# A per-sample 64x64 product with residual add: a laid-out x and result, whole-bank moves, held-back loads and block-diagonal products

## The chip, the cores and the metric

The kernel runs on one core of one Trainium2 chip. The metric is the device time of one execution in microseconds (us). Lower is better.

## What is computed

```python
def _L0_cond_ref(x, conditions, weights):
    w = weights[conditions]
    return jnp.einsum('bct,bcd->bdt', x, w)
x = x + _L0_cond_ref(x, itok_B_1_198, L0_cond_weights)
```

x is 64 x 64 x 512 float32 (samples B, channels C, times T: 8.39 MB), the table of weights is 200 x 64 x 64 float32, and itok_B_1_198 holds one table index per sample. Each sample's 64x512 matrix is multiplied by the transpose of its own 64x64 weight matrix and added to itself. Both kernels fold the addition into the product by adding the identity to each gathered weight matrix. So 8.39 MB of x and 1.05 MB of weights are read, and 8.39 MB are written.

## The kernel before

**Tiling.** Two samples make a pair (PAIR = 2): the first sits on partitions 0 to 63, the second on 64 to 127, by channel. There are 32 pairs. Four pairs make a turn, so there are TURNS = 8 turns. Half a turn (two pairs, 512 KB) is a round; there are 16 rounds, and each has one load and one store. All of x fits in `x_sb` and all of the result in `y_sb`, so no load waits for a buffer.

**Weights.** The sample indices are loaded as one row by a DMA that the ScalarE queue issues (L91). VectorE (DVE) spreads them over partitions with four 32x32 transposes (L133) and computes a table row for each partition (L137). GpSimd (POOL) issues one indirect DMA (L103), the gather, which brings 8 KB to each of 128 partitions into `gathered`. DVE adds the identity on the diagonals (L143) and transposes 32x32 blocks into `w_all` (L146). In L146 it reads `gathered` with a step of 64 elements. The semaphore `w_ready` then lets TensorE (PE) start.

**Turns.** For each pair PE makes two matmul calls (L119), one per half h of the partitions, each with 64 rows by 64 columns of the array: half h of `x_sb` times half h of `w_all`. Sample h of a pair goes to the product tile h, and g, the pair's parity, chooses the half of the product's partitions. So four calls of the two pairs g = 0, 1 use four different quarters of the array. A float32 call is two MATMUL instructions in the trace. There are two sets of product tiles (SETS = 2), each of two tiles of two banks. PE waits for the moves of the turn two before.

**Moves.** ScalarE (ACT, L95) copies product tile 0 to `y_sb` partitions 0 to 63, DVE (L152) copies tile 1 to partitions 64 to 127. Each does it in two instructions per turn, one for each half g of the product's partitions, so an instruction moves 64 partitions x 1024 elements.

**Order of the transfers.** SyncE (SP) issues all 16 loads first with no wait (L80), then for each turn waits for the moves of both engines (L83, L84) and issues two stores (L85). All loads and stores are on this one queue in this order. x and the result stand in DRAM sample by sample, so that a transfer of one partition's part of one pair is a run of 2 KB. The last wait is for all stores.

Of the kernel before, what the change touches and what calls it, by code (L numbers as in the profile page):

```python
# [3 lines left out]


def conditioned_residual_kernel(nc: bass.Bass, x: bass.AP, conditions: bass.AP, weights: bass.AP, out: bass.AP):
# [8 lines left out]
    fp32 = mybir.dt.float32  # L15
# [3 lines left out]
    B, C, T = x.shape  # L19
    S, _, D = weights.shape  # L20
    PAIR = 2
    P = PAIR * C
    PAIRS = B // PAIR
    Q = 32
    K = C // Q
    ROUNDS = PAIRS // 2
    TURNS = ROUNDS // 2
    SETS = 2

    x_rows = x.rearrange("(n two) c t -> (two c) n t", two=PAIR)  # L30
    out_rows = out.rearrange("(n two) c t -> (two c) n t", two=PAIR)
    condition_row = conditions.rearrange("b one -> one b")
    table = weights.rearrange("s (k c) d -> (s k) (c d)", k=K)

    ctx = ExitStack()
    with ctx:  # L36
# [13 lines left out]
        gathered = sbuf("gathered", [P, Q * D], fp32)  # L50
        w_all = sbuf("w_all", [P, D, PAIRS], fp32)

# [3 lines left out]
        x_loaded = [semaphore(f"x_loaded{m}") for m in range(ROUNDS)]  # L56
# [4 lines left out]
        rows_known = semaphore("rows_known")  # L61
        w_gathered = semaphore("w_gathered")
        identity_added = semaphore("identity_added")
        w_ready = semaphore("w_ready")
        multiplied = semaphore("multiplied")
# [8 lines left out]
        def slots_of(turn, g):  # L74
            return slice(4 * turn + g, 4 * turn + 4, 2)
# [12 lines left out]
        @block.scalar  # L88
        def _(act):
            act.wait_ge(condition_cleared, 1)  # L90
            act.dma_start(condition[0:1, :], condition_row).then_inc(condition_loaded, 16)  # L91
# [14 lines left out]

        @block.tensor
        def _(pe):
            pe.wait_ge(w_ready, 1)
            for turn in range(TURNS):  # L110
                if turn >= SETS:
                    pe.wait_ge(moved_by_act, 2 * (turn - SETS + 1))
                    pe.wait_ge(moved_by_dve, 2 * (turn - SETS + 1))
                for j in range(2):
                    pe.wait_ge(x_loaded[2 * turn + j], 16)
                    for g in range(2):
                        for h in range(PAIR):
                            n = 4 * turn + 2 * j + g
# [52 lines left out]
```

## Time and profile before

| | us |
|---|---|
| median of 3 runs | 51.25 |
| lowest, highest | 50.74, 51.54 |
| the profiled execution, its own time | 50.88 |
| its span, first to last instruction | 49.1 |
| busy DVE / ACT / PE / POOL in it | 24.8 / 17.4 / 17.5 / 1.6 |
| bytes moved by DMA | 17.84 MB |

The profile is of one execution. Its span begins at the first instruction and ends at the last; 1.8 us of the execution's own time lie outside the span. Busy times count computing instructions only. L12 is line 12 of the kernel. PEld is the loading of weights into TensorE. The DMA share is the mean busy share of the core's 16 DMA engines; packets of one engine can overlap, so it may be a little over 1.

### The profile page before, as it was taken

To read this page: it belongs to the slowest core of one execution; us is meant where nothing else is said; L and a number is where in the kernel's file an instruction comes from. 1 tells how busy PE (TensorE), PEld (TensorE's weight loads), DVE (VectorE), ACT (ScalarE), POOL (GpSimd) and SP (SyncE) were. 2 spreads that over 40 slices of the span, in tenths; PEclk is the share of its full clock that TensorE was granted. 3 is DMA by queue.
4 is the path that set the end of the run, shared out by engine and by line. 5 is a ranking of instruction groups with operands and counts; after the bars stand their busy time and mean duration, and the time that the engine had idled before them with its cause. 6 is when DMAs were issued, how large, how long until landed. Compare 5 with 4: busy or idle time off the path is not lost.

```text
span 49.1 us, 383 instructions
## 1 busy us (share of the span) xinstructions
PE 17.5 (36%) x128; PEld 7.0 (14%) x128; DVE 24.8 (50%) x28; ACT 17.4 (35%) x17; POOL 1.6 (3%) x9
## 2 busy tenths in 40 slices
PE   0000000000000069997495959696969300000000
PEld 0000000000000023240333334343424000000000
DVE  1043000000089930059999999999999997000000
ACT  0720000000000000059977878796969690000000
POOL 4003500000000000000000000000000000000000
PEclk9999999999999999999999999999999999555555
DMA  0399999999999999999999999999999999999950
GB/s 0 68 382 406 350 361 334 417 409 429 386 397 401 386 389 384 389 386 391 382 389 392 411 404 402 414 407 404 407 411 406 404 404 406 404 406 412 402 199 13
DMA packets 8851, 17.84 MB, mean 364 GB/s; under 512 B 530, under 2 KB 530, under 8 KB 8722
## 3 DMA queue, kind: packets, MB, share of 16 engines
q1 hardware_dynamic: 8704, 16.78, 90.7%
q0 software_dynamic: 144, 1.05, 5.1%
q8 instruction: 1, 0.02, 0.1%
q10 hardware_dynamic: 2, 0.00, 0.0%
HBM read 9.44 MB, written 8.39 MB: 363 GB/s over the span
## 4 chain that ended last, share of the span: by engine, by line
DVE 45%; DMA 19%; issue 8%; PE 8%; DVEq 3%; POOL 1%; POOLq 1%
DVE y_sb L152 37%; DMA gathered<-weights,table_row 19%; PE product L119 8%; DVE w_all L146 7%; DVEq L36 3%; POOL piece L101 1%; DVE gathered L143 1%; POOLq L36 0%; POOLq L161 0%
## 5 line engine op out<-in xcount | busy, mean ns | idle before, releaser
L119 PE MATMUL product<-x_sb,w_all 64*64 64x512 f32 x128 | 17.5, 669 | 21.0 <-DVE w_all L146 17.6
L95 ACT COPY y_sb<-product 64x1024 f32<-64x1024 f32 x16 | 16.1, 1007 | 21.7 <-PE product L119 21.5
L152 DVE COPY y_sb<-product 64x1024 f32<-64x1024 f32 x16 | 19.6, 1223 | 4.3 <-PE product L119 3.8
L119 PEld LDWEIGHTS product<-x_sb,w_all 64*64 64x64 f32 x128 | 7.0, 204 | 30.7 <-DVE w_all L146 17.6
L143 DVE TENSOR_TENSOR gathered<-gathered,piece 128x64 f32<-128x64 f32 x1 | 0.3, 268 | 9.4 <-DMA gathered<-weights,table_row 9.4
L146 DVE STREAM_TRANSPOSE w_all<-gathered 128x2048 f32<-128x2048 f32 x1 | 3.6, 3621 | 0.0
L95 ACT ACT_TABLE_LOAD x1 | 1.3, 1283 | 1.5 <-DVE condition L126 1.5
L133 DVE STREAM_TRANSPOSE condition_of<-condition 32x32 int32<-32x32 int32 x4 | 0.8, 202 | 1.8 <-DMA condition<-conditions 1.7
L103 POOL DMA_INDIRECT gathered<-weights,table_row x1 | 1.1, 1068 | 3.2 <-DVE table_row L137 3.2
L126 DVE MEMSET condition<- 32x64 int32 x1 | 0.1, 112 | 0.8 <-PEq L161 0.8
L101 POOL MEMSET piece<- 32x1 f32 x4 | 0.4, 91 | 0.5 <-POOLq L161 0.3
L128 DVE MEMSET piece<- 32x1 f32 x4 | 0.2, 59 | 0.2
L137 DVE TENSOR_SCALAR table_row<-condition_of,piece 128x1 int32<-128x1 int32 x1 | 0.2, 214 | 0.1
L161 POOL MEMSET const-uint8-127<- 128x1 uint8 x1 | 0.1, 128 | 0.0
L161 POOL MEMSET const-bfloat16-1.0<- 128x1 bf16 x1 | 0.1, 123 | 0.0
L161 POOL MEMSET const-float32-1.0<- 128x1 f32 x1 | 0.1, 114 | 0.0
L161 POOL MEMSET const-float32-0.0<- 128x1 f32 x1 | 0.1, 103 | 0.2 <-issue 0.2
## 6 DMA issues: line engine op xcount, KB each, us to landing
x_sb<-x SPq DMA_DIRECT2D x16, 512.0 KB, 11.2
out<-y_sb SPq DMA_DIRECT2D x16, 512.0 KB, 5.8
condition<-conditions ACTq DMA_DIRECT2D x1, 0.2 KB
gathered<-weights,table_row POOLq DMA_INDIRECT x1, 9.1
```

The source lines that it names most:

```text
L36: with ctx:
L95: nc.scalar.copy(y_sb[halves(0), slots_of(turn, g), :], product[turn % SETS][0][halves(g), :, :]).then_inc(moved_by_act, 1)
L101: nc.gpsimd.memset(piece[q * Q:(q + 1) * Q, 0:1], float(1 - q % K)).then_inc(pieces_set, 1)
L103: nc.gpsimd.indirect_dma_start(gathered[:, :], None, table, bass.IndirectOffsetOnAxis(ap=table_row[:, 0:1], axis=0),).then_inc(w_gathered, 16)
L119: product_of = nc.tensor.matmul(product[turn % SETS][h][halves(g), j, :], w_all[halves(h), :, n], x_sb[halves(h), n, :], start=True, stop= ...
L128: nc.vector.memset(piece[q * Q:(q + 1) * Q, 1:2], float(q % K)).then_inc(pieces_set, 1)
L133: nc.vector.transpose(condition_of[q * Q:(q + 1) * Q, :], condition[:, q // K:B:PAIR]).then_inc(condition_turned, 1)
L137: nc.vector.tensor_scalar(table_row[:, :], condition_of[:, 0:1], float(K), piece[:, 1:2], ALU.mult, ALU.add).then_inc(rows_known, 1)
L143: nc.vector.tensor_tensor(diagonal, diagonal, piece[:, :].unsqueeze(1).to_broadcast([P, Q, K]), ALU.add).then_inc(identity_added, 1)
L146: nc.vector.transpose(w_all[:, :, :], gathered[:, :].rearrange("p (c d) -> p d c", d=D)).then_inc(w_ready, 1)
L152: nc.vector.tensor_copy(y_sb[halves(1), slots_of(turn, g), :], product[turn % SETS][1][halves(g), :, :]).then_inc(moved_by_dve, 1)
L161: nc = bacc.Bacc("TRN2", target_bir_lowering=False, num_devices=1)
```

## The change

The arrays are now laid out by the caller. x comes as [128 partitions, 32 pairs, 512], so that the four pairs of a turn are one run of 8 KB in each partition's row of 64 KB, and the result leaves in the same form. The table's rows are stored with d outside and c inside, so that the block transpose into `w_all` reads `gathered` in its own order. In the device kernel:

- **Transfers.** One load and one store per turn (1 MB each), 8 and 8 instead of 16 and 16. SP issues two loads, then waits for `gather_started`, which POOL's issue of the gather sets, and then issues the other six.
- **Moves.** One instruction per engine and turn: ACT moves product tile 0 and DVE product tile 1, each 128 partitions x 1024 elements.
- **Products.** Turns 0 to 3 (TILED = 4) as before, two calls of 64x64 for each pair. Turns 4 to 7 take one call for each pair, with a 128x128 weight matrix `w_diag` that holds the two samples' matrices as diagonal blocks. Its two other blocks are set to zero early, one by POOL (L113) and one by DVE (L150). ACT fills the diagonal blocks for turn t + 4 with two copies (L101) ahead of its move of turn t.
- **Waits.** PE waits for x once per turn, and in turns 4 to 7 also for `w_zeroed` and `w_placed`.

The diff, cut to its core:

```diff
-            for m in range(ROUNDS):
-                sp.dma_start(x_sb[:, 2 * m:2 * m + 2, :], x_rows[:, 2 * m:2 * m + 2, :]).then_inc(x_loaded[m], 16)
-            for m in range(ROUNDS):
-                if m % 2 == 0:
-                    sp.wait_ge(moved_by_act, m + 2)
-                    sp.wait_ge(moved_by_dve, m + 2)
-                sp.dma_start(out_rows[:, 2 * m:2 * m + 2, :], y_sb[:, 2 * m:2 * m + 2, :]).then_inc(stored, 16)
-            sp.wait_ge(stored, 16 * ROUNDS)
+            for turn in range(TURNS):
+                if turn == EARLY:
+                    sp.wait_ge(gather_started, 1)
+                sp.dma_start(x_sb[:, pairs_of(turn), :], x[:, pairs_of(turn), :]).then_inc(x_loaded[turn], 16)
+            for turn in range(TURNS):
+                sp.wait_ge(moved_by_act, turn + 1)
+                sp.wait_ge(moved_by_dve, turn + 1)
+                sp.dma_start(out[:, pairs_of(turn), :], y_sb[:, pairs_of(turn), :]).then_inc(stored, 16)
+            sp.wait_ge(stored, 16 * TURNS)
...
             for turn in range(TURNS):
+                if turn < TILED:
+                    later = slice(4 * turn, 4 * turn + 4)
+                    act.wait_ge(w_ready, 1)
+                    for h in range(PAIR):
+                        nc.scalar.copy(w_diag[halves(h), later, h * D:(h + 1) * D],
+                                       w_all[halves(h), :, pairs_of(TILED + turn)].rearrange("p d n -> p n d")
+                                       ).then_inc(w_placed, 1)
                 act.wait_ge(multiplied, turn + 1)
-                for g in range(2):
-                    nc.scalar.copy(y_sb[halves(0), slots_of(turn, g), :], product[turn % SETS][0][halves(g), :, :]
-                                   ).then_inc(moved_by_act, 1)
+                nc.scalar.copy(y_sb[:, 4 * turn:4 * turn + 2, :], product[turn % SETS][0][:, :, :]
+                               ).then_inc(moved_by_act, 1)
...
+            pool.wait_ge(pieces_set, 2 * (P // Q))
+            nc.gpsimd.memset(w_diag[halves(1), :, 0:D], 0.0).then_inc(w_zeroed, 1)
             pool.wait_ge(rows_known, 1)
             nc.gpsimd.indirect_dma_start(gathered[:, :], None, table,
                                          bass.IndirectOffsetOnAxis(ap=table_row[:, 0:1], axis=0),
-                                         ).then_inc(w_gathered, 16)
+                                         engine_sem=gather_started).then_inc(w_gathered, 16)
...
             for turn in range(TURNS):
+                pe.wait_ge(x_loaded[turn], 16)
                 if turn >= SETS:
-                    pe.wait_ge(moved_by_act, 2 * (turn - SETS + 1))
-                    pe.wait_ge(moved_by_dve, 2 * (turn - SETS + 1))
+                    pe.wait_ge(moved_by_act, turn - SETS + 1)
+                    pe.wait_ge(moved_by_dve, turn - SETS + 1)
+                if turn == TILED:
+                    pe.wait_ge(w_zeroed, 2)
+                if turn >= TILED:
+                    pe.wait_ge(w_placed, PAIR * (turn - TILED + 1))
                 for j in range(2):
-                    pe.wait_ge(x_loaded[2 * turn + j], 16)
                     for g in range(2):
+                        n = 4 * turn + 2 * j + g
+                        if turn >= TILED:
+                            product_of = nc.tensor.matmul(product[turn % SETS][j][:, g, :], w_diag[:, n - 4 * TILED, :],
+                                                          x_sb[:, n, :], start=True, stop=True)
+                            continue
                         for h in range(PAIR):
...
+            nc.vector.memset(w_diag[halves(0), :, D:PAIR * D], 0.0).then_inc(w_zeroed, 1)
...
-            diagonal = bass.AP(gathered, 0, [[Q * D, P], [D + 1, Q], [Q, K]])
+            diagonal = bass.AP(gathered, 0, [[D * Q, P], [Q + 1, Q], [Q * Q, K]])
...
-            nc.vector.transpose(w_all[:, :, :], gathered[:, :].rearrange("p (c d) -> p d c", d=D)
+            nc.vector.transpose(w_all[:, :, :], gathered[:, :].rearrange("p (d c) -> p d c", d=D)
...
-                for g in range(2):
-                    nc.vector.tensor_copy(y_sb[halves(1), slots_of(turn, g), :], product[turn % SETS][1][halves(g), :, :]
-                                          ).then_inc(moved_by_dve, 1)
+                nc.vector.tensor_copy(y_sb[:, 4 * turn + 2:4 * turn + 4, :], product[turn % SETS][1][:, :, :]
+                                      ).then_inc(moved_by_dve, 1)
```

On SP, the transfers stood before in this order (`x_sb<-x` is a load of one round, `out<-y_sb` a store; the first rows of the queue, up to the third turn's stores):

```order
L80 DMA x_sb<-x 128x2x512 x16
L85 DMA out<-y_sb 128x2x512 [waits moved_by_dve,moved_by_act]
L85 DMA out<-y_sb 128x2x512
L85 DMA out<-y_sb 128x2x512 [waits moved_by_dve,moved_by_act]
L85 DMA out<-y_sb 128x2x512
```

and now all of them are these:

```order
L85 DMA x_sb<-x 128x2048 x2
L85 DMA x_sb<-x 128x2048 [waits gather_started]
L85 DMA x_sb<-x 128x2048 x5
L89 DMA out<-y_sb 128x2048 [waits moved_by_dve,moved_by_act] x8
```

Six of the eight loads moved behind the gather's issue; nothing else is on SP's queue between them.

On ACT, the queue between its table load and the turn-1 move was before (`product_0` is product tile 0 of either set):

```order
L95 ACT_TABLE_LOAD
L95 COPY y_sb<-product_0 64x2x512 [waits multiplied]
L95 COPY y_sb<-product_0 64x2x512
L95 COPY y_sb<-product_0 64x2x512 [waits multiplied]
L95 COPY y_sb<-product_0 64x2x512
```

and now it is, with the placing of weights ahead of each of the first four moves:

```order
L101 ACT_TABLE_LOAD
L101 COPY w_diag<-w_all 64x4x64 [waits w_ready]
L101 COPY w_diag<-w_all 64x4x64
L105 COPY y_sb<-product_0 128x1024 [waits multiplied]
L101 COPY w_diag<-w_all 64x4x64 [waits w_ready]
L101 COPY w_diag<-w_all 64x4x64
L105 COPY y_sb<-product_0 128x1024 [waits multiplied]
```

On PE, the last two turns are now (`x2` is two calls in a row on the same tile):

```order
L135 MATMUL product_0<-x_sb,w_diag 128x512 [waits moved_by_dve,w_placed,moved_by_act,x_loaded6]
L135 MATMUL product_0<-x_sb,w_diag 128x512
L135 MATMUL product_1<-x_sb,w_diag 128x512 x2
L135 MATMUL product_0<-x_sb,w_diag 128x512 [waits moved_by_dve,w_placed,moved_by_act,x_loaded7]
L135 MATMUL product_0<-x_sb,w_diag 128x512
L135 MATMUL product_1<-x_sb,w_diag 128x512 x2
```

Four calls of 128 partitions stand in each where eight calls of 64 partitions stood.

## Rows read from the trace of the kernel before

**Rows 1.** The page's second part: busy tenths in 40 slices.
```profile
DVE  1043000000089930059999999999999997000000
...
DMA  0399999999999999999999999999999999999950
GB/s 0 68 382 406 350 361 334 417 409 429 386 397 401 386 389 384 389 386 391 382 389 392 411 404 402 414 407 404 407 411 406 404 404 406 404 406 412 402 199 13
```
**Rows 2.** Busy time by stretch; the last three columns are granted clock, DMA share, GB/s.
```profile
2.00:5.00 3.00, 0.00 (x0) 0.00 (x0) 1.02 (x5) 0.78 (x1) 0.50 (x1) 1.00 0.96 352
5.00:9.00 4.00, 0.00 (x0) 0.00 (x0) 0.00 (x0) 0.00 (x0) 0.57 (x1) 1.00 1.00 352
9.00:13.00 4.00, 0.00 (x0) 0.00 (x0) 0.00 (x0) 0.00 (x0) 0.00 (x0) 1.00 1.02 414
14.00:24.00 10.00, 5.42 (x36) 1.80 (x36) 6.15 (x4) 2.58 (x3) 0.00 (x0) 1.00 1.05 390
28.00:38.00 10.00, 8.04 (x71) 3.58 (x64) 9.75 (x9) 8.02 (x9) 0.00 (x0) 1.00 1.05 407
...
47.00:48.00 1.00, 0.00 (x0) 0.00 (x0) 0.00 (x0) 0.00 (x0) 0.00 (x0) 0.50 0.30 115
```
**Rows 3.** The page's third part: DMA queues (q1 is SP's, q0 the gather's).
```profile
q1 hardware_dynamic: 8704, 16.78, 90.7%
q0 software_dynamic: 144, 1.05, 5.1%
```
**Rows 4.** The page's sixth part: issues, KB each, us to landing.
```profile
x_sb<-x SPq DMA_DIRECT2D x16, 512.0 KB, 11.2
out<-y_sb SPq DMA_DIRECT2D x16, 512.0 KB, 5.8
gathered<-weights,table_row POOLq DMA_INDIRECT x1, 9.1
```
**Rows 5.** Groups of instructions: count, busy us, mean ns, idle before and its releaser.
```profile
L152 DVE COPY y_sb<-product 64x1024 f32<-64x1024 f32 x16 | 19.6, 1223 | 4.3 <-PE product L119 3.8
L119 PE MATMUL product<-x_sb,w_all 64*64 64x512 f32 x128 | 17.5, 669 | 21.0 <-DVE w_all L146 17.6 <-issue 2.5 <-ACT y_sb L95 0.9
L95 ACT COPY y_sb<-product 64x1024 f32<-64x1024 f32 x16 | 16.1, 1007 | 21.7 <-PE product L119 21.5
...
L146 DVE STREAM_TRANSPOSE w_all<-gathered 128x2048 f32<-128x2048 f32 x1 | 3.6, 3621 | 0.0
...
L128 DVE MEMSET piece<- 32x1 f32 x4 | 0.2, 59 | 0.2
...
L126 DVE MEMSET condition<- 32x64 int32 x1 | 0.1, 112 | 0.8 <-PEq L161 0.8
```
**Rows 6.** The timeline: start us, duration us, engine, line, what.
```profile
0.75 0.53 POOL L101 MEMSET piece<- 32x1 f32 x4 [0.29 <-POOLq L161]
0.76 16.83 SPq L80 DMA_DIRECT2D x_sb<-x  x16
...
2.99 0.90 DVE L133 STREAM_TRANSPOSE condition_of<-condition 32x32 int32<-32x32 int32 x4 [1.69 <-DMA condition<-conditions]
...
4.50 1.07 POOL L103 DMA_INDIRECT gathered<-weights,table_row  x1 [3.22 <-DVE table_row L137]
13.66 0.27 DVE L143 TENSOR_TENSOR gathered<-gathered,piece 128x64 f32<-128x64 f32 x1 [9.44 <-DMA gathered<-weights,table_row]
```
**Rows 7.** The timeline of TensorE's first two turns.
```profile
17.64 5.37 PE L119 MATMUL product<-x_sb,w_all 64*64 64x512 f32 x32 [17.64 <-DVE w_all L146]
18.57 0.25 PEld L119 LDWEIGHTS product<-x_sb,w_all 64*64 64x64 f32 x4 [0.59 <-issue]
...
20.28 0.25 PEld L119 LDWEIGHTS product<-x_sb,w_all 64*64 64x64 f32 x4 [0.60 <-issue]
...
21.56 0.21 PEld L119 LDWEIGHTS product<-x_sb,w_all 64*64 64x64 f32 x4 [0.22 <-issue]
21.99 0.21 PEld L119 LDWEIGHTS product<-x_sb,w_all 64*64 64x64 f32 x4 [0.22 <-issue]
...
23.95 2.01 PE L119 MATMUL product<-x_sb,w_all 64*64 64x512 f32 x16 [0.94 <-ACT y_sb L95]
```
**Rows 8.** The chain that ended last: its share by line, and its last piece.
```profile
by line: DVE y_sb L152 37.4%; DMA gathered<-weights,table_row 18.6%; issue 7.9%; PE product L119 7.6%; DVE w_all L146 7.4%; DVEq L36 2.5%; POOL piece L101 0.7%; DVE gathered L143 0.6%; POOLq L36 0.5%; POOLq L161 0.0%
...
40.18 1.23 DVE y_sb L152
```

More of the change, by code:

```diff
@@ L3, with conditioned_residual_kernel @@
 from contextlib import ExitStack
-def conditioned_residual_kernel(nc: bass.Bass, x: bass.AP, conditions: bass.AP, weights: bass.AP, out: bass.AP):
+PAIR = 2
+def conditioned_residual_kernel(nc: bass.Bass, x: bass.AP, conditions: bass.AP, table: bass.AP, out: bass.AP):
     fp32 = mybir.dt.float32
@@ L17, in conditioned_residual_kernel @@
     ALU = mybir.AluOpType
[L19 to L23, printed above, removed]
+    P, PAIRS, T = x.shape
+    B = conditions.shape[1]
+    C = D = P // PAIR
     Q = 32
     K = C // Q
-    ROUNDS = PAIRS // 2
-    TURNS = ROUNDS // 2
+    TURNS = PAIRS // 4
     SETS = 2
[L30 to L33, printed above, removed]
+    EARLY = 2
+    TILED = TURNS // 2
     ctx = ExitStack()
@@ L49, in conditioned_residual_kernel @@
         table_row = sbuf("table_row", [P, 1], i32)
-        gathered = sbuf("gathered", [P, Q * D], fp32)
+        gathered = sbuf("gathered", [P, D * Q], fp32)
         w_all = sbuf("w_all", [P, D, PAIRS], fp32)
+        w_diag = sbuf("w_diag", [P, PAIRS - 4 * TILED, PAIR * D], fp32)
         product = [[ctx.enter_context(nc.psum_tensor(f"product{s}_{h}", [P, 2, T], fp32)) for h in range(PAIR)]
                    for s in range(SETS)]
-        x_loaded = [semaphore(f"x_loaded{m}") for m in range(ROUNDS)]
+        x_loaded = [semaphore(f"x_loaded{turn}") for turn in range(TURNS)]
         condition_loaded = semaphore("condition_loaded")
@@ L61, in conditioned_residual_kernel @@
         rows_known = semaphore("rows_known")
+        gather_started = semaphore("gather_started")
         w_gathered = semaphore("w_gathered")
@@ L64, in conditioned_residual_kernel @@
         w_ready = semaphore("w_ready")
+        w_zeroed = semaphore("w_zeroed")
+        w_placed = semaphore("w_placed")
         multiplied = semaphore("multiplied")
@@ L72, in halves, with pairs_of @@
             return slice(h * C, (h + 1) * C)
-        def slots_of(turn, g):
-            return slice(4 * turn + g, 4 * turn + 4, 2)
+        def pairs_of(turn):
+            return slice(4 * turn, 4 * turn + 4)
         @block.sync
         def _(sp):
-            for m in range(ROUNDS):
-                sp.dma_start(x_sb[:, 2 * m:2 * m + 2, :], x_rows[:, 2 * m:2 * m + 2, :]).then_inc(x_loaded[m], 16)
-            for m in range(ROUNDS):
-                if m % 2 == 0:
-                    sp.wait_ge(moved_by_act, m + 2)
-                    sp.wait_ge(moved_by_dve, m + 2)
-                sp.dma_start(out_rows[:, 2 * m:2 * m + 2, :], y_sb[:, 2 * m:2 * m + 2, :]).then_inc(stored, 16)
-            sp.wait_ge(stored, 16 * ROUNDS)
+            for turn in range(TURNS):
[7 more added lines that the diff above has]
+            sp.wait_ge(stored, 16 * TURNS)
         @block.scalar
@@ L161 @@
     nc = bacc.Bacc("TRN2", target_bir_lowering=False, num_devices=1)
-    arrays = {"x": np.ascontiguousarray(x),
-              "conditions": np.ascontiguousarray(itok_B_1_198).reshape(-1, 1),
-              "weights": np.ascontiguousarray(L0_cond_weights)}
+    B, C, T = x.shape
+    S, _, D = L0_cond_weights.shape
+    Q = 32
+    x_laid = np.asarray(x).reshape(B // PAIR, PAIR, C, T).transpose(1, 2, 0, 3).reshape(PAIR * C, B // PAIR, T)
+    table = np.asarray(L0_cond_weights).reshape(S, C // Q, Q, D).transpose(0, 1, 3, 2).reshape(S * (C // Q), D * Q)
+    arrays = {"x": np.ascontiguousarray(x_laid),
+              "conditions": np.ascontiguousarray(itok_B_1_198).reshape(1, B),
+              "weights": np.ascontiguousarray(table)}
     args = [nc.dram_tensor(name, a.shape, mybir.dt.from_np(a.dtype), kind="ExternalInput").ap()
             for name, a in arrays.items()]
-    out = nc.dram_tensor("out", x.shape, mybir.dt.float32, kind="ExternalOutput").ap()
+    out = nc.dram_tensor("out", x_laid.shape, mybir.dt.float32, kind="ExternalOutput").ap()
     conditioned_residual_kernel(nc, *args, out)
     result = run_bass_kernel_spmd(nc, [arrays], core_ids=[0])
-    return result.results[0]["out"]
+    laid = np.asarray(result.results[0]["out"])
+    tiled = laid[:, :B // 4].reshape(2, D, B // 16, PAIR, 2, T).transpose(2, 4, 0, 3, 1, 5).reshape(B // 2, D, T)
+    whole = laid[:, B // 4:].reshape(PAIR, D, B // 4, T).transpose(2, 0, 1, 3).reshape(B // 2, D, T)
+    return np.concatenate([tiled, whole])
```

3 lines of the change are left out of this document (1 added, 2 removed).

## The prediction, made before the changed kernel ran

> **What bounds the kernel now.** I read the slices first. The reader should see two lines [rows 1]: the DMA engines are at nine tenths or more from the third slice to the thirty-eighth, while DVE, the busiest engine, has a hole of many slices before 21 us and is done six slices before the end. The stretches put numbers on it [rows 2]: the share is 0.96 to 1.05 in every stretch, with 390 GB/s where only loads run (14 to 24 us) and 407 GB/s where only stores run (28 to 38 us). 17.84 MB have to pass, and they pass without a gap from about 2 to 47.3 us (the 115 KB of 47 to 48 us are 0.3 us at 407 GB/s, and a thin tail follows).
>
> The chain of waits seems to say something else: DVE's moves have 37% of it and the gather 19% [rows 8]. But its last piece ends at 41.4 us, 7.7 us before the span does. Behind it the stores still queue: a store takes 5.8 us from issue to landing [rows 4] although its 512 KB need only 1.3 us at 407 GB/s. So the chain shows the second limit. DVE needs two moves of 1.22 us plus gaps, 2.5 us per turn [rows 5], and the DMA engines need 1.05 MB / 407 = 2.6 us per turn. A stream that gets faster than 418 GB/s (1.05 MB in 2.5 us) would meet DVE next. PE has 2.0 us of matmuls in a turn [rows 7]. The stream of DMA sets the end, DVE stands right behind it, PE behind that.
>
> **Part 1, 8 KB runs.** This is the term that decides. The loads and stores are 8,192 packets of 2 KB (8704 less 16 for each of 32 issues), and their packets took 90.7% of 16 engines' span: 0.907 x 16 x 49.1 us / 8192 = 87 ns each, 348 ns for four. The gather has 128 packets of 8 KB (144 less 16) at 5.1%: 0.051 x 16 x 49.1 / 128 = 313 ns each [rows 3]. An 8 KB packet costs a tenth less than four of 2 KB. Packet times overlap, so a rate is the safer measure. The gather landed at 4.5 + 9.1 = 13.6 us [rows 4, 6], and just before that, from 9 to 13 us, the rate was 414 GB/s against 390 later [rows 2]. I place its bytes in these four us: 1.05 of 1.66 MB in 8 KB packets. If the other 37% ran at 390, the 8 KB part ran at 430. So the new rate lies between 414 (what was seen with part of the traffic in long packets) and 430 (all of it). Today loads and stores need 8.39/390 + 8.39/407 = 21.5 + 20.6 = 42.1 us. At 414 they need 40.5, at 430 39.0. The sides beyond: no gain (42.1), and 10% off by the packet times (38.1). I take 422, in the middle, as the stores have less left to gain than the loads: 39.8 us, a gain of 2.3 us.
>
> The Trainium skill has a figure between the two lengths: its page "DMA: Bandwidth & Descriptors", section "SWDGE vs HWDGE vs iDMA", gives 408.7 GB/s for loads issued from SP in 4 KiB rows. Our 2 KB row has 390; by both, a fixed cost for each packet, an 8 KB packet would run at about 418 GB/s (an estimate), and the two directions would need 40.1 us, a gain of 2.0. No run here shows the 4 KB rate.
>
> **Part 2, whole-bank moves.** 16 moves of 1.22 us on DVE become 8; ACT's 16 of 1.01 us become 8 [rows 5]. Partitions are worked on side by side, so I price a 128x1024 move like a 64x1024 one; the trace has no other, and twice as long would be as before, 2.5 us per turn. This gives nothing by itself, since the stream hides the moves, but it takes away the 418 GB/s ceiling. Without it part 1 would be worth at most 42.1 - 40.1 = 2.0.
>
> **Part 3, held-back loads.** SP now waits for the gather's issue, which ends at 4.50 + 1.07 = 5.57 us [rows 6]. Behind the waiting instruction on SP stand six loads, and later all stores. The two early loads are 2.1 MB; by the slices [rows 1] 2.1 MB have passed at 8 us, with long runs perhaps at 7.4. The first held load is issued at 5.6, and the first one of all needed 1.1 us from issue (0.76) to flow, so it flows at 6.7: no hole, 0 us. The bound on the other side is a start signal that comes only when the gather itself begins to flow. As placed above, the gather began to flow at about 9.0. A hole from 7.4 to 9.0 is 1.6 us. I take 0, because the signal is set at the end of an instruction whose duration is in the timeline.
>
> What it brings is an earlier `w_ready`. The gather landed behind some 3 MB of queued loads; with 1 MB left ahead of it at 5.6 us it should land at about 11, between 8.1 (issue end plus 2.5 us of bytes) and 13.6 (as now). This is worth nothing in the stream, which carries the same bytes, but PE starts earlier, and part 5 needs this.
>
> **Part 4, setting up.** The block transpose of 3.62 us now reads in order. Its sides are 3.6 and 2.4 (2048 elements at the 1.19 ns per element of a DVE move, 1223/1024 [rows 5]); I take 3.0. The DVE memset of 1024 elements goes by 59 ns for 1 element and 112 for 64, 0.84 ns each: 0.9 us, in the 1.69 us in which DVE waits for the indices [rows 5, 6]. POOL's memset starts at 1.3 us and has until 4.5, a cover of 3.2 us [rows 6]. No row prices it; past 3.2 us it would delay the gather and the six held loads by the excess. PE starts at 11 + 0.5 + 0.3 + 3.0 = 14.8 instead of 17.6.
>
> **Part 5, block diagonals.** In the first turns weight loads come every 0.85 us, four at a time, and from 21.1 us every 0.43 us [rows 7]: four quarter-array matmuls run side by side, and PE's steps halve after 3.5 us of work, though the granted clock reads 1.00 in both. That is the 1.2 GHz level first and 2.4 GHz after. A turn of 16 instructions is four steps, 1.7 us, 2.0 with its ends. A block-diagonal turn has 8 instructions, and each fills the array, so nothing runs beside it: 8 x 0.43 = 3.4 us, 1.4 more than now. The call count falls and PE's work rises. PE: 14.8 + 3.7 (first turn, slow) + 3 x 2.0 + 4 x 3.4 = 38.1. The last move (1.25) and the start of the store (1.1) put the last store's data at 40.5. The new stream wants it when all else has passed: 47.3 - 2.3 - 2.5 (1.05 MB at 422) = 42.5. Cover: 2.0 us. ACT in the first four turns: one move 1.0 and two placings of 256 elements each, between 0.25 (by elements) and 1.0 (like a move); I take 0.4, 1.8 us per turn, under PE's 2.0. At 1.0 each it is 3.0 per turn, three us later in all, which would eat the cover and cost 1.
>
> **The sum.** Runs -2.3, all else 0 behind the stream. The profiled execution: span 49.1 - 2.3 = 46.8, own time 50.88 - 2.3 = 48.6. The median of the runs lies 0.37 above the profiled one, so 48.95; the stretch 5 to 9 us at 352 GB/s [rows 2], 0.4 us below the 390 pace, may improve with fewer loads queued, and I count half of it: 48.75, given as 48.8.
>
> **Rivals.**
> 1. *The hole.* The start signal comes late. For it: SP's queue has nothing else to give the engines, and the gather took 3.4 us from the end of its issue to flow. Against it: the issue ends in the trace at 5.57. Forecast + 1.6: 50.4, which is inside 2%.
> 2. *PE becomes the bound.* The gather lands as late as now and ACT's or DVE's set-up is slow, so PE starts at 17.6: 17.6 + 3.7 + 6.0 + 13.6 = 40.9, + 1.25 + 1.1 = 43.3 against 42.5 wanted: 0.8 us of idle engines in the last turn. 49.6. For it: only 2.0 us of cover. Against: fewer loads ahead of the gather.
> 3. *The length of the run does little.* The stream is held by bytes and not by packets, or the queue cuts runs into 2 KB again, so the change doesn't do what it says. For it: stores already have 407. Against: the 414 of the mixed stretch. 51.0 to 51.3.
> 4. *Slower: the rows' distance.* Each load now takes 128 runs that lie 64 KB apart, where before a pair was one block of 256 KB. If rows at equal steps meet in the same part of the memory, the loads fall to the slowest rate seen over a long stretch, 352 GB/s [rows 2]: 8.39/352 = 23.8 against 21.5, stores as now: 51.25 + 2.3 = 53.6. It decides from where both directions need over 43.1 us, a mean of 389 GB/s. Against it: the gather's scattered 8 KB rows ran well. The Trainium skill, "DMA: Bandwidth & Descriptors", section "Latency and other measured facts", lists copies by row pitch: 207 GB/s at 512 KiB, 164 at 2 MiB, 103 at 4 MiB, 214 with padding. By that trend a pitch of 64 KiB loses little, at most the 3% of 512 KiB, which would be 41.0 us for the two directions at 422 and leave 1.1 of the gain. No trace here shows it.
>
> **Chances.** Forecast 0.56 (its own range 47.8 to 49.8); hole 0.12; PE bound 0.10; run length does little 0.14; rows' distance, or another loss in the stream, 0.08. A measurement of this kernel tells about 2% from no change, that is 50.2 and 52.3. Faster: 0.56 + 0.10 + a third of the hole + a sixth of rival 3 for a partial gain = 0.72. Slower: 0.07. Same: 0.21. The range goes from 47.4 (430 GB/s, 3.1 less, the dip gone, and some) to 50.8, into rival 3.
>
> **What would show it.** Packets on SP's queue fall from 8,704 to about 2,300 with 8 KB each; right if the stretches of loads and of stores read 414 to 430 GB/s, wrong if either stays at 390 and 407. DMA share with no dip between 6 and 10 us: no hole; a dip names rival 1. The gather's issue to landing near 6.5 us instead of 9.1. The transpose at 2.4 to 3.6 us; PE starting near 14.8; moves of 128x1024 at 1.2 us; L135 steps of 0.43 us. DMA idle between the last two stores would name rival 2. The forecast is wrong as a whole if the span is outside 45.8 to 48.

## The result and the profile after

The changed kernel takes 48.67 us (median of 4 runs, 48.16 to 49.66) against 51.2 before (50.74 to 51.54). The ratio is 0.950 with a 95% interval of 0.938 to 0.963, so it is faster by 2.6 us. 48.8 was forecast. Executions of one kernel fall into a faster and a slower group; the medians here are of all executions, the ratios are of the faster group alone.

The profiled execution of the changed kernel is the longest of its four, 49.66 us with a span of 47.0. The page's parts on the stream, under [rows 1] and [rows 3]:

```profile
DMA  0689999999999999999998999999999999999950
GB/s 0 105 335 440 440 426 188 356 398 426 426 447 426 440 398 426 433 447 426 412 384 293 440 426 433 426 433 412 426 440 433 426 426 412 433 440 433 426 251 7
DMA packets 2450, 17.83 MB, mean 380 GB/s; under 512 B 274, under 2 KB 274, under 8 KB 274
## 3 DMA queue, kind: packets, MB, share of 16 engines
q1 hardware_dynamic: 2304, 16.78, 86.3%
q0 software_dynamic: 144, 1.05, 6.8%
```

Packets are down to a quarter and 8 KB long, and most slices read around 427. Two places do not: the seventh and eighth slices (188, 356) and the 21st and 22nd (384, 293). The same is seen in a second execution of the same kernel, that of run e1 below, which took 48.73 us. As it is the more typical one, its stretches are shown here, under [rows 2] (the last two columns are DMA share and GB/s):

```profile
2.00:7.00 5.00, 0.00 (x0) 0.00 (x0) 1.51 (x6) 0.77 (x1) 1.39 (x2) 1.00 0.95 383
7.00:10.00 3.00, 0.00 (x0) 0.00 (x0) 0.00 (x0) 0.00 (x0) 0.00 (x0) 1.00 1.00 347
10.00:24.00 14.00, 9.06 (x65) 3.59 (x65) 6.61 (x6) 6.97 (x10) 0.00 (x0) 1.00 1.01 425
24.00:26.00 2.00, 2.00 (x5) 0.97 (x6) 0.87 (x1) 1.95 (x3) 0.00 (x0) 1.00 0.95 307
26.00:44.00 18.00, 11.92 (x28) 4.94 (x26) 4.90 (x4) 4.25 (x5) 0.00 (x0) 0.93 1.01 428
```

In this execution loads run at 425 (was 390) and stores at 428 (was 407). At 428 the two directions need 39.2 us, 2.9 less than the 42.1 of before. The two dips give back (428 - 347) x 3 / 428 = 0.6 and (428 - 307) x 2 / 428 = 0.6 us. Note the share: it stays at 0.95 and 1.00 in the dips. The engines have packets in hand, but each takes longer: the trace also has a record of each packet (queue, start, duration, size), and by these records of e1 an 8 KB packet takes 0.31 us in the stores after 30 us, and on average 0.47 and 0.44 us in the two dips, up to 0.95. A reader who looked only at the DMA share would not see them. The execution of 49.66 us has the same dips, 303 GB/s at 7 to 10 us and 344 at 24 to 26.

The groups of the changed kernel, under [rows 5] (count, busy us, mean ns, idle before and its releaser):

```profile
L139 PE MATMUL product<-x_sb,w_all 64*64 64x512 f32 x64 | 8.9, 704 | 15.0 <-DVE w_all L168 14.9
L173 DVE COPY y_sb<-product 128x1024 f32<-128x1024 f32 x8 | 9.8, 1224 | 14.9 <-PE product L135 9.4
L135 PE MATMUL product<-x_sb,w_diag 128*128 128x512 f32 x32 | 14.0, 594 | 0.3 <-issue 0.3
L105 ACT COPY y_sb<-product 128x1024 f32<-128x1024 f32 x8 | 8.1, 1012 | 11.1 <-PE product L135 8.7
L101 ACT COPY w_diag<-w_all 64x256 f32<-64x256 f32 x8 | 5.1, 635 | 12.3 <-DVE w_all L168 12.1
...
L168 DVE STREAM_TRANSPOSE w_all<-gathered 128x2048 f32<-128x2048 f32 x1 | 2.3, 2311 | 0.0
...
L150 DVE MEMSET w_diag<- 64x1024 f32 x1 | 0.9, 912 | 0.3 <-issue 0.3
L113 POOL MEMSET w_diag<- 64x1024 f32 x1 | 1.0, 957 | 0.1
```

A move of 128 partitions costs what one of 64 did (1224 against 1223 ns). The transpose that reads in order takes 2.3 us, not 3.6. The block diagonals are 14.0 us of PE for four turns, 3.5 each. The timeline of the set-up, under [rows 6] and [rows 7]:

```profile
3.88 0.90 DVE L155 STREAM_TRANSPOSE condition_of<-condition 32x32 int32<-32x32 int32 x4 [1.40 <-DMA condition<-conditions]
...
5.39 1.08 POOL L115 DMA_INDIRECT gathered<-weights,table_row  x1 [3.07 <-DVE table_row L159]
12.21 0.27 DVE L165 TENSOR_TENSOR gathered<-gathered,piece 128x64 f32<-128x64 f32 x1 [7.10 <-DMA gathered<-weights,table_row]
...
14.88 9.04 PE L139 MATMUL product<-x_sb,w_all 64*64 64x512 f32 x64 [14.88 <-DVE w_all L168]
```

The indices arrive 0.9 us later than before (3.88 against 2.99), so the gather is issued 0.9 later. It lands 6.8 us after its issue instead of 9.1, at 12.2 us, and PE starts at 14.9 instead of 17.6.

### The profile page after: what moved, and what is told of

Same layout as the page of the kernel before. It is cut to its first block, busy times and chain, and to the rows that moved or that the text cites. A ratio compares the mean times of both kernels' runs of the same rounds, so it can differ in the third digit from the quotient of the medians.

```text
span 47.0 us, 301 instructions
## 1 busy us (share of the span) xinstructions
PE 22.9 (49%) x96; PEld 9.4 (20%) x96; DVE 14.6 (31%) x21; ACT 14.5 (31%) x17; POOL 2.6 (6%) x10
## 3 DMA queue, kind: packets, MB, share of 16 engines
q0 software_dynamic: 144, 1.05, 6.8%
## 4 chain that ended last, share of the span: by engine, by line
PE 49%; DMA 14%; DVE 9%; issue 8%; POOL 2%; POOLq 1%
PE product L135 30%; PE product L139 19%; DMA gathered<-weights,table_row 14%; DVE w_all L168 5%; DVE y_sb L173 3%; POOL w_diag L113 2%; DVE gathered L165 1%; POOLq L33 1%; DVE piece L148 0%; DVE condition L146 0%
## 5 line engine op out<-in xcount | busy, mean ns | idle before, releaser
L139 PE MATMUL product<-x_sb,w_all 64*64 64x512 f32 x64 | 8.9, 704 | 15.0 <-DVE w_all L168 14.9
L173 DVE COPY y_sb<-product 128x1024 f32<-128x1024 f32 x8 | 9.8, 1224 | 14.9 <-PE product L135 9.4
L135 PE MATMUL product<-x_sb,w_diag 128*128 128x512 f32 x32 | 14.0, 594 | 0.3 <-issue 0.3
L105 ACT COPY y_sb<-product 128x1024 f32<-128x1024 f32 x8 | 8.1, 1012 | 11.1 <-PE product L135 8.7
L101 ACT COPY w_diag<-w_all 64x256 f32<-64x256 f32 x8 | 5.1, 635 | 12.3 <-DVE w_all L168 12.1
L135 PEld LDWEIGHTS product<-x_sb,w_diag 128*128 128x128 f32 x32 | 6.0, 190 | 8.3 <-issue 8.3
L139 PEld LDWEIGHTS product<-x_sb,w_all 64*64 64x64 f32 x64 | 3.4, 205 | 19.7 <-DVE w_all L168 14.9
L168 DVE STREAM_TRANSPOSE w_all<-gathered 128x2048 f32<-128x2048 f32 x1 | 2.3, 2311 | 0.0
L150 DVE MEMSET w_diag<- 64x1024 f32 x1 | 0.9, 912 | 0.3 <-issue 0.3
L113 POOL MEMSET w_diag<- 64x1024 f32 x1 | 1.0, 957 | 0.1
```

Source lines behind the costliest of these rows:

```text
L101: nc.scalar.copy(w_diag[halves(h), later, h * D:(h + 1) * D], w_all[halves(h), :, pairs_of(TILED + turn)].rearrange("p d n -> p n d")).the ...
L105: nc.scalar.copy(y_sb[:, 4 * turn:4 * turn + 2, :], product[turn % SETS][0][:, :, :]).then_inc(moved_by_act, 1)
L113: nc.gpsimd.memset(w_diag[halves(1), :, 0:D], 0.0).then_inc(w_zeroed, 1)
L135: product_of = nc.tensor.matmul(product[turn % SETS][j][:, g, :], w_diag[:, n - 4 * TILED, :], x_sb[:, n, :], start=True, stop=True)
L139: product_of = nc.tensor.matmul(product[turn % SETS][h][halves(g), j, :], w_all[halves(h), :, n], x_sb[halves(h), n, :], start=True, stop= ...
L150: nc.vector.memset(w_diag[halves(0), :, D:PAIR * D], 0.0).then_inc(w_zeroed, 1)
```

## The experiments

There are twelve runs in three groups of four, on three chips, each group beside the kernel before. Ratios are to the kernel before in the same group, which has medians of 51.48, 51.05 and 51.95 us in the three. A difference of ratios is turned into us with 51.2. Times inside a run come from one profiled execution.

### First group: what the parts are worth

**e1, the changed kernel again.** No edit.

> The changed kernel once more, as the yardstick for the others of this call. Both theories: 48.7 us, 428 GB/s in the stretches of loads alone and stores alone, a dip of the stream at 7 to 9 us.

48.76 us, ratio 0.950 (0.940 to 0.960). As expected, with both dips.

**e2, no hold.**

```diff
-    EARLY = 2
+    EARLY = TURNS
```

> All eight loads issued at once, as before the change; all else as changed. The changed kernel's stream has a dip between 7 and 10 us that costs some 0.9 us. Theory 'the hold makes the dip': the stream is full there and the time falls by 0.9 to about 47.8, and the gather lands at 13 us or later. Rival 'the gather itself slows the stream whatever else is queued' (before had 352 GB/s in 5 to 9 us): the dip is about as large, 48.7, and the hold is worth nothing for the time.

49.49 us, ratio 0.966 (0.958 to 0.974): 0.8 us *longer* than e1. The intervals just overlap (e1 reaches to 0.960), so the size is uncertain, but the holes that cause it can be seen. The first theory was right about the dip and wrong about the time. Its slices:

```profile
DMA  0689999999999999999999999999999894792991
GB/s 0 110 345 427 393 441 427 434 434 420 441 427 413 420 427 427 420 434 413 413 427 420 427 434 420 406 413 441 427 434 406 344 386 172 331 441 110 420 386 76
```

Both dips are gone: it is above 390 from the fourth slice to the thirty-first. But now there are holes near the end. The gather lands 10.4 us after issue, so PE starts at 18.4 and each of the last turns takes 3.4 us on PE, while the stream needs 2.45 for a turn. SP issues the last four stores 3.43 us apart, the last at 43.3 us instead of 39.3. In this kernel the block diagonals are the bound at the end, and the hold is what buys their cover. (Cover is the time by which a result is ready before the stream wants it.)

**e3, 2 KB runs.** x and result lie pair by pair; the transfers are as large and as few as in the changed kernel. The store is changed in the same way as the load shown.

```diff
-                sp.dma_start(x_sb[:, pairs_of(turn), :], x[:, pairs_of(turn), :])
+                sp.dma_start(x_sb[:, pairs_of(turn), :], x.rearrange("n p t -> p n t")[:, pairs_of(turn), :])
```

> x and result in DRAM pair by pair, so that transfers have 2 KB runs again; still 1 MB for each transfer, hold and the rest as changed. Theory 'the length of the run sets the rate': 390 GB/s for loads and 407 for stores, 2.9 us longer than the changed kernel, about 51.5. Rival 'fewer and larger transfers or the other parts gave the gain': below 49.5.

52.07 us, ratio 1.015 (1.004 to 1.026): 3.3 us longer than e1, and 0.8 longer than the kernel before. Loads and stores alone (14 to 24 and 30 to 44 us):

```profile
14.00:24.00 10.00, 7.64 (x52) 2.81 (x56) 4.76 (x3) 5.01 (x7) 0.00 (x0) 1.00 1.05 391
...
30.00:44.00 14.00, 9.96 (x24) 4.11 (x22) 4.60 (x4) 3.75 (x4) 0.00 (x0) 1.00 1.05 408
```

These are the rates of [rows 2], 390 and 407, with all else in the device kernel as changed. The length of the run, with the layout that belongs to it, sets the rate; with 2 KB runs the size of a transfer (1 MB here, 512 KB before) does not. The rates explain 2.9 of the 3.3 us.

**e4, 8 KB runs alone** on the kernel before: the new layout of x and result, one load and one store per turn, nothing else.

```diff
-            for m in range(ROUNDS):
-                sp.dma_start(x_sb[:, 2 * m:2 * m + 2, :], x_rows[:, 2 * m:2 * m + 2, :]).then_inc(x_loaded[m], 16)
+            for turn in range(TURNS):
+                sp.dma_start(x_sb[:, 4 * turn:4 * turn + 4, :], x[:, 4 * turn:4 * turn + 4, :]).then_inc(x_loaded[turn], 16)
```

> The kernel before with nothing changed but the layout of x and result and 8 KB runs (one load and one store per turn). Theory 'the run length is nearly all of it, the rest is cover': 428 GB/s; the last store's data would start at 42.5 us (last DVE move ends 41.4, plus 1.1) against 42.0 wanted by the stream, so up to 0.5 us late: 48.3 to 48.9. Rival 'DVE's two moves per turn (2.5 us) cap the stream at 418 GB/s': stores below 420 and the time 49.2 or more.

51.65 us, ratio 1.005 (0.992 to 1.018): **no gain is seen**. The first theory was wrong. The rival named the right rate of the stores (413, under 420), but a cap at 418 alone would leave 2.0 us of gain. The stretches of its trace show the first reason:

```profile
17.00:24.00 7.00, 4.39 (x24) 1.55 (x28) 3.17 (x2) 0.61 (x1) 0.00 (x0) 1.00 1.01 420
24.00:27.00 3.00, 2.23 (x24) 0.93 (x20) 2.94 (x3) 2.93 (x4) 0.00 (x0) 1.00 0.32 134
27.00:45.00 18.00, 11.07 (x92) 4.55 (x84) 16.02 (x14) 12.58 (x13) 0.00 (x0) 0.97 1.01 413
```

The loads run at 420 and are over before 25 us. Then the engines are only 0.32 busy for three us, a loss of (428 - 134) x 3 / 428 = 2.1 us. The timeline shows what they wait for:

```profile
3.72 0.90 DVE L131 STREAM_TRANSPOSE condition_of<-condition 32x32 int32<-32x32 int32 x4 [2.42 <-DMA condition<-conditions]
...
5.23 1.07 POOL L101 DMA_INDIRECT gathered<-weights,table_row  x1 [3.95 <-DVE table_row L135]
15.63 0.27 DVE L141 TENSOR_TENSOR gathered<-gathered,piece 128x64 f32<-128x64 f32 x1 [10.68 <-DMA gathered<-weights,table_row]
...
19.61 5.59 PE L117 MATMUL product<-x_sb,w_all 64*64 64x512 f32 x32 [19.61 <-DVE w_all L144]
...
25.96 17.86 SPq L83 DMA_DIRECT2D out<-y_sb  x8
```

Only the loads and stores were edited, and what runs beside them came later: the indices land 0.7 us later than in [rows 6], the gather needs 10.4 us instead of 9.1. PE starts at 19.6 instead of 17.6 and the first store is issued at 26.0 instead of 23.9. The last load ends 1.7 us earlier than before on its first engine (24.6 against 26.3) and the first store comes 2.0 later. From there DVE's moves, 2.5 us a turn, hold the stores at 413 GB/s.

The gather's part comes from the long packets. By the packet records its 1.05 MB flow from 9.0 to 13.1 us in the kernel before, from 10 to 12 us at about 335 GB/s with x at 86 beside it, close to the 4 to 1 of the packet lengths (8 KB and 2 KB). In e4 they flow from 9.5 to 14.9, at about 230 with x at 200. The indices' part does not come from the length alone: in e3, with 2 KB runs in 1 MB transfers, they land at 3.60 us, 0.6 later than before. Whether the larger transfers do it was not tried by itself.

The second reason stands at the end of its slices:

```profile
GB/s 0 99 368 421 421 427 421 434 434 427 427 421 421 421 421 421 421 421 427 322 0 217 414 421 421 421 421 421 421 421 421 421 394 414 421 421 421 224 26 7
```

Fifteen of the 16 DMA engines have ended the last store at 47.0 us, one ends it at 49.1. This last engine decides the time, and it costs 2.1 us in this execution. What it does is told under e6.

### Second group: which cover, and where the dips come from

**e5, quarters in all turns**: TILED = TURNS, and everything of `w_diag` is taken out (the two memsets, the eight placings, its waits).

> The changed kernel with all eight turns by 64x64 quarters (no block diagonals, no placing, no zeroing). Theory 'the diagonals are hidden work': PE ends some 6 us earlier, the span is the same within 0.3 us, 48.7. It also tells whether the second dip of the stream, at 24 to 26 us, comes from the diagonals' start (then it is gone and the time is 0.4 us less) or from the switch from loads to stores after the hold (then it stays).

48.61 us, ratio 0.955 (0.946 to 0.964), the same as e1's 0.950 within the intervals. PE is done at 30 us instead of 38, and nothing changes. With the hold, the block diagonals are hidden work: no cost and no gain is seen. Both dips stay (312 and 283 in their slices), so the dip at 24 us is not from the block diagonals.

**e6, no hold and quarters in all turns**: e5 with EARLY = TURNS (all eight loads issued at once).

> No hold and no block diagonals, whole-bank moves and 8 KB runs kept. With no hold the changed kernel had a full stream up to 37 us and then two holes, each after a turn of diagonals (3.4 us a turn on PE). Theory 'without the hold the diagonals are the bound': with quarters a turn is 2.0 us, the holes are gone, no dip at 7 to 9 us either, so 17.83 MB at 427 GB/s in one piece: span 45.3 to 45.6, time 47.5 to 47.8, the fastest so far. Rival 'the first store comes too late, as in the run of 8 KB runs alone': a hole at 25 us and 48.7 or more.

48.45 us (47.63 to 48.88), ratio 0.941 (0.930 to 0.951). The stream is full as expected, but the span of this profile is 47.0, not 45.5:

```profile
GB/s 0 91 328 433 426 419 426 419 447 426 433 412 426 426 433 433 412 412 433 426 419 412 433 433 426 433 426 412 433 426 433 412 412 426 426 440 426 286 28 7
...
q8 instruction: 1, 0.02, 0.1%
```

The last slices read 286, 28, 7. One engine's share of 428 GB/s is 27: a single engine still works for 1.4 us when fifteen are done. By the landings, all 16 engines ended each store within 0.6 us until 36 us, and from the store that ended at 37 to 39 us on, one engine was 1.4 us behind. In between, from 37.2 to 38.1 us, one engine carried the 16 KB instruction fetch of queue q8. The same stands in e4 (fetch at 39.5 us, one engine 2.1 us late from the next store on), e7, e11 and e12. The records do not name the engine, so that the late one is the one with the fetch is read from the times, five times out of five.

**e7, moves split again** on e6, two of 64 partitions x 1024 per engine and turn.

```diff
-                nc.vector.tensor_copy(y_sb[:, 4 * turn + 2:4 * turn + 4, :], product[turn % SETS][1][:, :, :]
-                                      ).then_inc(moved_by_dve, 1)
+                for g in range(2):
+                    moved = nc.vector.tensor_copy(y_sb[halves(g), 4 * turn + 2:4 * turn + 4, :], product[turn % SETS][1][halves(g), :, :])
+                moved.then_inc(moved_by_dve, 1)
```

> As the run before, but each move split again in two of 64 partitions x 1024. Theory 'DVE's two moves of 1.22 us cap the stores at 2.5 us per turn': stores come every 2.5 us against 2.45 of the stream, and the first store is 1.2 us later and so misses the end of the loads by about 1 us: 48.5 to 49.1. Rival 'the width of the moves does not matter for the time': as the run before.

49.78 us, ratio 0.976 (0.969 to 0.983): 1.8 us longer than e6 by the ratios, 1.3 by the medians, somewhat more than expected. The first store is issued at 24.3 us (23.0 in e6), and most later ones 2.49 us apart; its slices read 210 and 325 between 24 and 28 us. One engine was again late at the end, by 1.9 us, after an instruction fetch at 35.7. The late engine is in both, so without a hold the whole-bank moves are worth 1.3 to 1.8 us.

**e8, three loads ahead of the hold.** EARLY = 3.

> The changed kernel with three loads ahead of the hold instead of two. The gather began to flow at 7.0 us, just as the two early loads ran dry, and the held loads only at 9.75, 3.4 us after their issue. Theory 'the dip is the gather starting with an empty engine beside it': with 3.1 MB early the stream is full to 9.2 us, the dip is gone (0.7 to 0.9 us less), the gather lands 2 us later and PE's cover of 2.5 us is just enough: 47.9 to 48.2. Rival 'the gather starts slowly whenever it is alone': the dip moves to 9 to 11 us and the time stays at 48.7.

49.22 us, ratio 0.959 (0.948 to 0.970). The dip at 7 to 9 us is gone and did not move, so the first theory is right on that. But the gather lands 10.1 us after issue, as with no hold, and the diagonals leave the same holes at the end as in e2. With three loads ahead of it, the hold hardly brings the gather forward (10.1 us against the 10.4 of e2).

### Third group: the best version

**e9, the changed kernel.**

> The changed kernel as the yardstick of this call: 48.7 us, a dip at 7 to 9 us and one at 24 to 26 us.

48.62 us, ratio 0.943 (0.935 to 0.951). As expected, with both dips (290 and 361, 375 and 325 GB/s in their slices).

**e10, e6 again.**

> No hold, quarters in all turns, once more beside the changed kernel. Its stream was full, but one of the 16 DMA engines finished each store 1.4 us after the others from the point on where that engine also carried a 16 KB instruction fetch (37.2 to 38.1 us). Theory 'a full stream is worth 1.2 to 1.6 us and the fetch takes most of it back': 48.0 to 48.4, and in an execution whose fetch falls outside the stream 47.5. Rival 'no real difference from the changed kernel': both at 48.7.

48.19 us, ratio 0.931 (0.920 to 0.941), the lowest in both groups in which this kernel ran. It beats the changed kernel by 0.4 us in medians and 1.3% in ratios, but the intervals overlap, so this is likely and not shown. The profiled execution took 47.41 us, and in it the instruction fetch fell behind the stream:

```profile
GB/s 0 108 331 410 417 445 424 424 424 445 410 424 438 424 424 424 417 424 424 417 424 424 431 424 417 431 431 424 424 431 424 431 424 424 431 417 445 417 309 0
```

No dip and no tail: 309, then 0. This is the fullest stream of all profiles, span 45.6. By stretches, loads, the switch, and stores:

```profile
15.00:24.00 9.00, 6.00 (x44) 2.53 (x48) 4.56 (x4) 1.77 (x2) 0.00 (x0) 1.00 1.01 422
24.00:27.00 3.00, 3.00 (x36) 1.47 (x32) 2.00 (x3) 1.58 (x3) 0.00 (x0) 1.00 1.02 426
27.00:44.00 17.00, 6.54 (x64) 3.06 (x56) 5.81 (x5) 4.76 (x5) 0.00 (x0) 0.83 1.01 428
```

**e11, a later first store** on e5 (the first three stores all wait for the third turn's moves).

```diff
-                sp.wait_ge(moved_by_act, turn + 1)
-                sp.wait_ge(moved_by_dve, turn + 1)
+                sp.wait_ge(moved_by_act, max(turn + 1, 3))
+                sp.wait_ge(moved_by_dve, max(turn + 1, 3))
```

> Quarters in all turns, hold as changed, and SP waits for the moves of the third turn before its first store (about 22.5 instead of 19.0 us). The dip at 24 to 26 us stood in the runs whose first store was issued at 19 to 19.4 us and not in those with 23 us or later. Theory 'stores that wait long in the queue behind loads slow the last load': the dip is gone, 0.4 to 0.6 us less than the quarters with hold (48.6), so 48.0 to 48.2. Rival 'the dip belongs to the hold (the engines run out of step after it)': it stays, 48.6.

49.08 us (48.66 to 50.76), ratio 0.953 (0.946 to 0.961), no gain. The experiment missed. Its profiled execution is the longest of the six, 50.76 us, and stands for the others only in part: in it the gather landed 2 us later than in e5, and the first store was issued at 25.5, when 14 of 16 engines had ended the last load. Its slices:

```profile
GB/s 0 114 348 422 428 422 295 408 415 428 422 428 428 428 428 428 408 428 422 428 181 214 428 415 415 402 422 408 388 422 422 428 428 428 428 408 422 355 27 7
```

Up to 24.5 us the last load ran undisturbed (422, 428), and behind it came a hole (181, 214). So it fits that early-queued stores slow the last load, but a hole took the place of the dip here, and nothing was won. The cause of the dip at 24 to 26 us stays open.

**e12, two and a half loads ahead of the hold** on e5.

> Quarters in all turns, two and a half loads ahead of the hold (the third load in two halves of 4 KB runs). Theory 'the gather begins when the early loads run dry, or some 3 us after its issue': it begins at 8.4 us, the stream has a smaller dip (0.3 us instead of 0.9), and the time is 48.0 to 48.3. Rival 'a gather that starts alone is slow for 2 us whenever that is': the same loss, 48.6.

48.87 us, ratio 0.952 (0.946 to 0.957), no different from e5. The slices:

```profile
GB/s 0 118 306 437 444 444 333 451 427 340 420 416 430 430 423 430 430 437 402 430 326 416 423 423 430 430 423 430 416 423 416 430 430 437 430 416 423 389 42 7
...
q8 instruction: 1, 0.02, 0.1%
```

The gather began to flow at 8.6 us, when the early loads ran dry, as the first theory has it. The first dip is only a little smaller (333 and 340 in single slices; 400 GB/s over 6 to 12 us, against 389 in e5, which is 0.2 us, where 0.6 was hoped for). The second stays (326), and one engine ends 1.2 us after the others (42, 7), with a fetch inside the stream at 31.4 us. The late engine took back more than the smaller dip gave, if it is there in every execution; one was profiled.

## Why the prediction came out

The time was right to 0.1 us, and that closeness is luck. The main step, a faster stream through longer runs, was right; several errors of 0.6 to 0.9 us around it cancelled.

**Right.** The stream of DMA was the bound. It was right to take the rate from the stretch in which the gather's 8 KB packets ran: by the packet records they flowed from 9.0 to 13.1 us, where the prediction had placed them. The upper end of the bracket came out, 428 against 430, and 422 was chosen. Gain 2.9 where 2.3 was put. An estimate from the figure for 4 KiB rows in the Trainium skill, "DMA: Bandwidth & Descriptors", section "SWDGE vs HWDGE vs iDMA", as a fixed cost per packet, gave 418; the trace has 425 and 428, so it was low by 2%. Rival 4, the rows' distance, did not come: 64 KB apart, the runs go at 425 and 428. The same page of the Trainium skill, section "Latency and other measured facts", has its smallest row pitch at 512 KiB; the loss of up to 3% that the prediction allowed by its trend is not seen at 64. Of the pieces on the engines most came out as priced: move 1.22 (1.2), DVE memset 0.91 (0.9), block diagonals 3.5 us a turn (3.4), transpose 2.3 (3.0, with 2.4 as its lower side). A placing on ACT took 0.64 where 0.4 was taken, so ACT needs 1.0 + 2 x 0.64 = 2.3 us in a turn, over PE's 2.0; e1's stores of turns 1 to 3 are issued 2.1 to 2.4 us apart. PE's start at 14.9 (14.8) is luck: the indices came 0.9 us later and the gather took 0.3 more, against 0.7 less for the transpose and 0.5 in the sum ("11 + 0.5") that no row shows. Rival 2 was right not to be the forecast: SP waited for the last store's landing 6.5 us in e1, and its 1 MB needs 2.5, so there was cover.

**Wrong in part 3, "so it flows at 6.7: no hole, 0 us".** The start signal was not late by itself (SP issued at 6.50, just after the gather's issue ended at 6.47), so rival 1's mechanism did not occur. But the gather's issue came 0.9 us later than in before, and the held loads did not flow 1.1 us after theirs. By the packet records of e1 the early loads ran dry at 7.5 us, the gather alone was on the engines from 7.5 to 9.9, rising from 150 to 426 GB/s, and the first held load flowed from 9.9, 3.5 us after its issue. The 1.1 us was the delay of a queue on idle engines. The trace of before had the other figure too: the gather's 3.4 us from the end of its issue to flow. I had used it for the rival only. Cost: 0.6 us. The sign named for a hole, a dip of the DMA share, would have missed it: the share is 1.00 there. And the 0.2 us that the forecast counted for the slow stretch of before (352 GB/s at 5 to 9 us) did not come with the hold; only without it is the stretch full (e2).

**Not foreseen: the dip at 24 to 26 us.** Another 0.6 us. With 8 KB runs it comes with the hold (after, e1, e5, e9, e12) and is absent where the gather came as late as with no hold (e2, e6, e8, e10), whatever PE does; with the hold and 2 KB runs (e3) it is absent too, though there also the first store was issued over 5 us before the loads ended.

**Right by the sum: 2.9 - 0.6 - 0.6 + about 0.9.** The last part is a remainder. Its largest piece is the end: before, the engines ended the last store between 47.0 and 48.4 us, the last one 1.0 after the mean; in e1 between 45.1 and 45.8, the last one 0.4 after the mean. That is 0.7, and it was not in the forecast. The slow stretch of before is another 0.4, and some 0.2 went lost elsewhere.

**Wrong in "Runs -2.3, all else 0 behind the stream", and too generous in part 2, "Without it part 1 would be worth at most 2.0".** By e4, part 1 alone shows no gain. The check I made of cover was at the last store only. The first store counts just as much: it must be there when the loads end, and faster loads end sooner. In before, the first store was issued at 23.9 and the last load ended at 26.3 to 27.5; in e4 it was issued at 26.0 and the last load ended at 24.6 to 25.0. And I had left out what long packets do to the gather beside them, and the late engine. From e4 the other parts can be followed, roughly one at a time. The runs are of different groups, and e7 also has another order in `y_sb` than e4. The late engine falls into some profiles and not into others. So beside the ratio the table has the times at which the fifteenth and the last of the 16 DMA engines ended the last store, in us, of one execution each:

| kernel | ratio | step | 15th, last engine |
|---|---|---|---|
| before | 1 | | 48.0, 48.4 |
| e4: 8 KB runs only | 1.005 | 0 | 47.0, 49.1 |
| e7: + transpose in order | 0.976 | -1.5 us | 45.8, 47.7 |
| e6, e10: + whole-bank moves | 0.941, 0.931 | -1.8 us | 44.8, 46.2 and 44.6, 44.8 |
| e5: + hold of six loads | 0.955 | +0.7 us (intervals overlap: not shown) | 45.5, 45.6 |
| e1, e9: + block diagonals | 0.950, 0.943 | 0 | 45.7, 45.8 and 45.6, 45.6 |

By the fifteenth engine the 8 KB runs alone do bring 1.0 us, the transpose another 1.2, the moves 1.0, and the hold takes back 0.7 to 0.9. So the gain of the 8 KB runs alone is hidden twice, by the hole at 24 to 27 us and by the late engine.

So the change is 8 KB runs (3.3 us when taken away, e3), which show in full only because the transpose and the moves bring the first store forward by about 3 us (26.0 in e4, 23.0 in e6). The hold also brings it forward (19.4 in e1), at the price of the two dips, and then more cover is there than is used. The block diagonals are not needed for the time, and without the hold they cost 1.3 us (e2 against e6). What they may do is keep the instruction fetch out of the stream, which was not tried by itself.

## What to carry to other kernels

When a transfer stream is the bound and gets faster, look for its cover at both ends: the first result must be ready when the last load ends, as well as the last result when the stores run out. A part that is worth nothing on the old kernel (a faster transpose, wider moves) can be what lets another part pay. And longer packets on a bulk queue took share from the gather beside them (1.3 us in e4), so a transfer that starts the chain of work should be looked at together with the bulk. Last, read the end of a stream engine by engine: one late engine of 16 can hide what the other fifteen have won.

## What the runs showed of the hardware

- Runs of 2 KB go at 390 (loads) and 407 GB/s (stores), runs of 8 KB at 425 and 428 (e1). With 2 KB runs, transfers of 512 KB and of 1 MB go at the same rates (before, e3).
- Long x packets take more of an engine beside another queue. The gather's 8 KB packets moved at about 335 GB/s beside 2 KB packets at 86, and at about 230 beside 8 KB ones at 200, so it landed 9.1 us after its issue in before and 10.4 us in e4. The indices landed 0.6 to 0.9 us later in the changed kernels, but by 0.6 also with 2 KB runs (e3), so this is not shown to be the packets' length.
- A move of 128 partitions x 1024 elements takes what one of 64 takes: 1.22 us on DVE and 1.01 on ACT (after and before). The DVE block transpose of 2048 elements takes 2.3 us when it reads in order and 3.6 with a step of 64 elements (after and before).
- A transfer that was issued while another queue kept the engines busy began to flow only some 3 us later. For the gather this is 3.1 to 3.5 us from the end of its issue (before, e2, e4, e6, e7, e8, e10). For the held loads it is 3.5 to 3.6 us from their issue in after, e1, e5, e9 and e12, and 2.5 in e3 and e11. On idle engines it is 1.0 to 1.1 (the first load). Where the bulk queue ran dry earlier, the gather began right then (7.2 us in e1, 8.6 in e12).
- A 16 KB instruction fetch that falls into the stream of 8 KB packets goes with one engine of 16 lagging by 1.2 to 2.1 us from then to the end, and the last engine decides. It was inside the stream in e4, e6, e7, e11 and e12 and outside in e5 and e10, all seven with quarters in all turns. In before it was inside too (39.4 us), but there the last engine was only 0.1 to 0.3 us behind the next. None of the profiles with block diagonals, which have 32 fewer matmul instructions, had it inside (after, e1, e2, e3, e8, e9). Whether the number of instructions decides when the fetch comes was not tried.
